# Taking the first expert layer's results back: stores by slot and gathers by pairs of columns in place of scatters and four block loads

## The chip, the cores and the metric

The kernel runs on one core of a Trainium2 chip. The metric is the device time of one execution in microseconds, the median of three runs. TensorE (PE), VectorE (DVE), ScalarE (ACT), GpSimd (POOL) and the DMA queues each work through their own list of instructions in order and wait for each other by semaphores, all of them written out by hand.

## What is computed

```python
h = concat([patches(x) @ proj_w.T + proj_b + pos, segment + sinusoid + token rows])   # 8 x 192 rows of 192
h = h + rotor_scan(layernorm(h))                          # a recurrence over the 192 positions
h = h + moe(layernorm(h), 8 experts, top 2, hidden 288, gelu)          # "experts(0)"
h = h + linear_attention(layernorm(h), 12 heads of 16)                 # relu(q), relu(k), k^T v, no softmax
h = h + moe(layernorm(h), 8 experts, top 2, hidden 768, silu)          # "experts(1)"
```

The 1536 token rows stand in SBUF as 12 columns of 128 rows: columns 0 to 3 hold the 64 image rows of two batch items each, columns 4 to 11 the 128 text rows of one item each. The attention of one item needs half an image column and one text column, so one "trio" (image column i, text columns 4 + 2i and 5 + 2i) is what two items need; there are four trios. `trio(i)` names them.

## The kernel before

**First experts.** `route(0)` on DVE gives each of the 3072 pairs (token row, chosen expert) a slot number. The slots are grouped by expert into 31 tiles of 128. POOL gathers a tile's rows from DRAM by an index list (`gather`, L738), PE transposes them, multiplies by the expert's two matrices, ACT applies the gelu, and DVE copies the result out of PSUM into one of eight buffers `ys` (`evac_y`, L1571). POOL then scatters the 128 result rows (`scatter`, L746) to the DRAM tensor `expert_rows` at the place of their token: choice 1 in the first 1536 rows, choice 2 in the next. On POOL's list gather and scatter alternate.

**Results back.** `load_acc` waits for all scatters and reads the rows back in token order with plain DMAs, four blocks of columns (`ACC`: 2, 2, 4 and 4 columns), choice 1 into `xn` on SP's queue and choice 2 into `a1` on ACT's. Behind its half, SP's queue holds the loads of the second experts' weights (L611 to L614, 9.4 MB). DVE multiplies both by the gates and adds them to `h` (L1630, two instructions a column), takes the statistics of the layer norm (`ln_start`, L1177 and L1180; `ln_end`, L1196 and L1197), ACT takes the square root (L821) and normalises (L834).

**Attention.** It works on six pairs of columns and four trios. For a pair, PE transposes the rows (`t_pair`, L1854), ACT copies them out (L1088), PE computes keys and values (`kv_mms`, L2229 and L2235), which DVE (`k_evac`, L1642) and ACT (`v_evac`, L1098) copy out; queries are computed for two pairs at a time (`q_mms`, L2261 and L2266, copied out by DVE in `q_evac`, L1650). For a trio there are the sums k^T v (`sums`, L2283 and L2289; DVE's `state`, L1660), numerator and denominator (`numden`, L2305 and L2310; DVE's `ratio`, L1673 to L1678), the transposes of the result (`t_att`, L2317; ACT's `att_evac`, L1118) and the output projection (`out_proj`, L2338; DVE's `add_att`, L1712 to L1180). The pairs go in the order of the columns, so the first text columns are the third pair, and the first `sums` stands behind the transposes of all six pairs. PE's list is written out at the end of `build`, DVE's above it.

**Behind it.** The next layer norm, the routing of the second layer on DVE and the 31 tiles of the second experts follow; POOL gathers and scatters there too. `keep_busy(n, b)` is n matmuls of 128x512 in bf16 whose result is not used (L1803).

## Time and profile before

| what | value |
|---|---|
| median of 3 runs (457.75 to 463.28) | 462.23 us |
| profiled execution, its own time | 462.79 us |
| its span, first to last instruction | 461.0 us |
| mean granted TensorE clock | 0.956 of full |
| busy: PE, DVE, ACT, POOL | 91%, 63%, 43%, 49% |
| first experts, first gather to last copied result | 137.5 to 230.9 us |
| results back and attention, to the end of the last projection | 230.9 to 298.6 us |
| layer norm and routing, to the first transposed row of the second experts | 298.6 to 320.8 us |
| second experts and the end | 320.8 to 461.0 us |

Times inside the execution are microseconds from the start of the span. In a row of the timeline the first number is the start, the second the duration; "x8" merges eight instructions that follow one another; the bracket at the end is the time for which the engine was idle before, and what ended it. SPq and ACTq rows are DMA issues.

### The profile page before, as it was taken

How to read it: one execution, taken by the hardware profiler on the slowest of the kernel's cores; microseconds unless marked ns; L12 is line 12 of the kernel's file. 1: busy time of each engine (PE TensorE's matmuls, PEld its weight loads, DVE VectorE, ACT ScalarE, POOL GpSimd, SP SyncE). 2: the span in 40 equal slices, each digit the busy share in tenths (PEclk: the TensorE clock that was granted, in tenths of full speed). 3: DMA queues.
4: the chain of work that ended last, by engine and by line, in shares of the span. 5: the costliest groups of instructions: out<-in, count | busy, mean ns of one | idle time of the engine just before them, and what ended most of it. 6: DMA issues, size and time to landing. Idle time of an engine off the chain costs nothing.

```text
span 461.0 us, 10231 instructions
## 1 busy us (share of the span) xinstructions
PE 420.2 (91%) x3568; PEld 326.3 (71%) x3568; DVE 292.3 (63%) x1360; ACT 197.3 (43%) x374; POOL 225.6 (49%) x266
## 2 busy tenths in 40 slices
PE   7999998989788988989987988977999999999993
PEld 5653655637536877878844557933999999999993
DVE  6579999999782433333558336887465566556651
ACT  1287945441751111110123401546566566566660
POOL 4302798797035666666520000334456665665544
PEclk9799799999989999898979999998999999999998
DMA  8609400010132122222169999079233233333322
GB/s 233 96 1 227 113 0 3 1 35 1 58 102 70 60 61 70 69 70 70 47 195 236 224 225 217 15 137 139 50 62 50 54 62 63 51 55 61 51 25 27
DMA packets 40128, 39.02 MB, mean 85 GB/s; under 512 B 7575, under 2 KB 37259, under 8 KB 40079
## 3 DMA queue, kind: packets, MB, share of 16 engines
q1 hardware_dynamic: 28861, 23.05, 22.5%
q0 software_dynamic: 9312, 14.03, 15.3%
q10 hardware_dynamic: 1906, 1.30, 1.0%
q8 instruction: 29, 0.48, 0.4%
q14 instruction: 20, 0.16, 0.1%
HBM read 28.00 MB, written 11.06 MB: 85 GB/s over the span
## 4 chain that ended last, share of the span: by engine, by line
PE 66%; DVE 11%; DMA 10%; ACT 4%; POOL 4%; issue 4%; POOLq 1%; SPq 0%; DVEq 0%; another core or an unknown queue 0%; ACTq 0%
PE bank L1955 11%; PE bank L1990 10%; PE bank L1941 7%; PE bank L1983 7%; DMA out<-a,idx 5%; PE bank L2036 4%; POOL reg L707 3%; PE bank L1803 3%; PE bank L1964 2%; DMA xn<-expert_rows 2%; PE bank L1918 2%; ACT xn L834 2%; DMA reg<-xn_rows,idxs 1%; PE bank L2229 1%; DMA reg<-in_patchT 1%
## 5 line engine op out<-in xcount | busy, mean ns | idle before, releaser
L738 POOL DMA_INDIRECT reg<-xn_rows,idxs x62 | 60.5, 976 | 30.3 <-issue 16.6
L1955 PE MATMUL bank<-reg,xT 64*128 64x128 f32 x1116 | 72.6, 275 | 1.4 <-issue 1.1
L758 POOL DMA_INDIRECT out<-a,idx x31 | 50.3, 1622 | 46.7 <-DMA out<-a,idx 35.8
L1955 PEld LDWEIGHTS bank<-reg,xT 64*128 64x128 f32 x1116 | 68.6, 188 | 1.5 <-issue 1.0
L1990 PE MATMUL bank<-reg 64*128 64x192 f32 x744 | 69.0, 323 | 0.0
L1990 PEld LDWEIGHTS bank<-reg 64*128 64x128 f32 x744 | 63.4, 187 | 0.0
L1803 PE MATMUL bank<-con 128*128 128x512 bf16 x201 | 55.3, 435 | 0.0
L1045 ACT ACTIVATE reg<-reg 128x1152 f32 x31 | 36.1, 1163 | 30.8 <-PE bank L1990 30.8
L1574 DVE TENSOR_SCALAR a<-bank,gs 128x192 f32<-128x192 f32 x31 | 13.0, 418 | 53.2 <-PE bank L1990 53.2
L1024 ACT ACTIVATE reg<-bank 128x288 f32<-128x288 f32 x31 | 12.5, 410 | 77.4 <-PE bank L1941 62.9
L746 POOL DMA_INDIRECT expert_rows<-a,idx x31 | 30.6, 986 | 25.2 <-DVE a L1571 19.1
L1803 PEld LDWEIGHTS bank<-con 128*128 128x128 bf16 x201 | 21.6, 111 | 27.6 <-issue 12.0
L1941 PE MATMUL bank<-reg,xTs 96*128 (+1 forms) x124 | 36.7, 418 | 4.8 <-DVE xTs L1537 4.7
L1983 PE MATMUL bank<-reg 96*128 x186 | 36.9, 336 | 0.3 <-issue 0.3
L1571 DVE COPY a<-bank 128x192 f32<-128x192 f32 x31 | 11.0, 354 | 39.6 <-PE bank L1983 20.6
L1983 PEld LDWEIGHTS bank<-reg 96*128 96x128 f32 x186 | 32.8, 195 | 3.7 <-issue 0.8
L1547 DVE TENSOR_SCALAR reg<-bank,gb 128x128 f32<-128x128 f32 x93 | 32.3, 403 | 0.0
L787 POOL TENSOR_SCALAR onep<-rs 128x3 f32<-128x3 f32 x4 | 0.9, 228 | 57.2 <-DVE nm L1189 57.2
L1941 PEld LDWEIGHTS bank<-reg,xTs 96*128 96x128 f32 (+1 forms) x124 | 21.8, 196 | 9.8 <-issue 6.2
L707 POOL TENSOR_TENSOR reg<-reg 128x128 f32<-128x128 f32 x63 | 26.1, 457 | 5.1 <-PE bank L2110 4.9
L1028 ACT ACTIVATE reg<-bank 128x384 f32<-128x384 f32 x31 | 15.2, 490 | 21.7 <-PE bank L1955 13.4
L1309 DVE TENSOR_REDUCE bank<-reg 128x6 f32<-128x24 f32 x176 | 23.9, 181 | 0.0
(363 smaller groups left out, 800.9 us busy)
## 6 DMA issues: line engine op xcount, KB each, us to landing
reg<-in_w2b SPq DMA_DIRECT2D x8, 576.0 KB, 10.2
reg<-in_w1b SPq DMA_DIRECT2D x8, 288.0 KB, 10.4
reg<-in_w1a SPq DMA_DIRECT2D x8, 216.0 KB
reg<-in_w2a SPq DMA_DIRECT2D x8, 216.0 KB
xn_rows<-xn SPq DMA_DIRECT2D x4, 384.0 KB, 2.7
reg<-in_w1b SPq DMA_DIRECT2D x8, 192.0 KB, 8.5
xn_rows<-xn SPq DMA_DIRECT2D x1, 1152.0 KB, 7.8
out<-h SPq DMA_DIRECT2D x1, 1152.0 KB
```

Of the source, the lines that this page charges most:

```text
L707: ins = nc.gpsimd.tensor_tensor(term[b % 2][k][:, 0:n, :, r, :], second[:, :, :, r, k:k + 1].to_broadcast([P, n, NCH, 4]), first[:, :, :, ...
L738: pool.indirect_dma_start(xs[:, i % RING, 0:(D, D2)[l]], None, xd[l], bass.IndirectOffsetOnAxis(ap=idxs[:, i:i + 1], axis=0)).then_inc(xs_ ...
L746: pool.indirect_dma_start(ybuf, bass.IndirectOffsetOnAxis(ap=idx2[:, i:i + 1], axis=0), ys[:, i % YRING, :], None).then_inc(scat[i % YRING ...
L758: pool.indirect_dma_start(out, bass.IndirectOffsetOnAxis(ap=idx2[:, i:i + 1], axis=0), ys[:, i % YRING, :], None, compute_op=ALU.add).then ...
L1045: nc.scalar.activation(w2r[:, p, :], w2b.rearrange("p e c n -> p (e c n)")[:, bass.ds(e * W2R, W2R)], ACT.Copy).then_inc(w2r_act, 1)
L1309: V.tensor_reduce(slot(t)[:, ch, 0:3], entries[:, ch], AX, ALU.add).then_inc(scan_self[half], 1)
L1547: ins = V.tensor_scalar(dst[:, k], src[:, :, 64 * k:64 * k + 64], gb2[:, 0, k:k + 1], gb2[:, 1, k:k + 1], ALU.mult, ALU.add)
L1803: MM(bank[bk][:, :], con[:, 0:P // 2].bitcast(BF16), con[:, 0:2 * P].bitcast(BF16), start=True, stop=True)
L1941: ins = MM(bank[2 + p][:, 0:hid], xTs[0:r, p, k, :], w1v[0:r, bass.ds(e * (NK * hid) + k * hid, hid)], start=(k == 0), stop=(k == NK - 1))
L1955: ins = MM(bank[2 + 2 * p + a][:, c * P:(c + 1) * P], w1r[rs, p, col:col + hc], xT64[rs, p, k, :], start=(c == 0 and k == 0), stop=(c == n ...
L1983: ins = MM(bank[6 + p][:, 0:D], hTs[0:r, p, c * P:(c + 1) * P], w2v[0:r, bass.ds(e * (nhc * D) + c * D, D)], start=(c == 0), stop=(c == nh ...
L1990: ins = MM(bank[Y_BANKS[i == NT - 1][a]][:, 0:D], hT2[rs, p, c * P:(c + 1) * P], w2r[rs, p, c * D:(c + 1) * D], start=(c == 0), stop=(c == ...
```

## The change

- `expert_rows` is now laid out by slot: tile i of the first experts is stored whole, 128 rows in a piece, by SP (a plain DMA for each of the 31 tiles, each waiting for `y_ev`). POOL's list in this layer holds the 31 gathers alone. The weight loads stand behind the stores on SP's queue.
- `load_acc` on SP and ACT goes. `results_back(n)` on POOL gathers the results of pair n by the slot numbers (`sli`), four indirect DMAs a pair (two columns, two choices), 24 in all. Pairs 2 to 5 first wait until the transposed rows of pair n - 2 have been copied out (`xT_ready`). Two of POOL's memsets stand between them.
- The pairs now go in batch order (`ORDER`): trio 0 is pair 0 and half of pair 1, and so on. `xn`, `a1`, `att`, `kb`, `vb`, `qT` and `attT` are indexed by that order.
- On PE, DVE and ACT the attention is written out anew: each pair's keys, each trio's sums and projections come as soon as their pairs are there. Keys and values of all pairs share banks 2 and 3; queries and sums share banks 4 and 5; the queries of the last two pairs are computed one pair at a time (`Q_PAIRS`), so there are four `q_mms` where there were three. PE has 12 more `keep_busy` matmuls after the landing of the first pair's last gather, and four after its first keys.
- The rows of the second layer's input are stored in two steps of six DMAs each in place of two DMAs.

```diff
-        ybuf = nc.dram_tensor("expert_rows", [TOPK * NTOK + 32 * P, D], F32, kind="Internal").ap()
+        ybuf = nc.dram_tensor("expert_rows", [NT * P, D], F32, kind="Internal").ap()
...
+        ND_BANK = [(6, 7), (6, 7), (6, 7), (2, 3)]
+        PR_BANK = [(6, 7), (6, 7), (6, 7), (4, 5)]
+
+        Q_PAIRS = ((0, 2), (2, 2), (4, 1), (5, 1))
...
+        ORDER = [j for i in range(NBP) for j in trio(i)]
+        GROUPS[3] = [ORDER[2 * n:2 * n + 2] for n in range(NPAIR)]
...
-            load_acc(sp, 0)
+
+            for i in range(NT):
+                sp.wait_ge(y_ev, i + 1)
+                sp.dma_start(ybuf[i * P:(i + 1) * P, :], ys[:, i % YRING, :]).then_inc(y_st[i % YRING], 16)
...
+            for i0, i1 in ((0, NBP - 1), (NBP - 1, NBP)):
+                sp.wait_ge(xn5_ready, 3 * i1)
+                of = xn[:, 3 * i0:3 * i1, :].rearrange("p (i v) n -> p i v n", v=3)
+                pat = slice(i0, i1)
+                for c, n in ((slice(0, D), D), (slice(D, DX), DX - D)):
+                    sp.dma_start(tok_rows(xd[1])[:, pat, c], of[:, :, 0, 0:n]).then_inc(xd_written, 16)
+                    for a in range(2):
+                        sp.dma_start(tok_rows(xd[1])[:, NPJ + 2 * i0 + a:NPJ + 2 * i1:2, c],
+                                     of[:, :, 1 + a, 0:n]).then_inc(xd_written, 16)
...
-                    if l == 0:
-                        pool.indirect_dma_start(ybuf, bass.IndirectOffsetOnAxis(ap=idx2[:, i:i + 1], axis=0),
-                                                ys[:, i % YRING, :], None).then_inc(scat[i % YRING], 16)
-                        return
...
+            def results_back(n):
+
+                for q in (2 * n, 2 * n + 1):
+                    for k, buf in enumerate((xn, a1)):
+                        a, g = k * NJ + ORDER[q], 2 * q + k
+                        if g >= YRING:
+                            pool.wait_ge(scat[g % YRING], 16 * (g // YRING))
+                        pool.indirect_dma_start(buf[:, q, :], None, ybuf,
+                                                bass.IndirectOffsetOnAxis(ap=sli[:, 0, a:a + 1], axis=0)
+                                                ).then_inc(scat[g % YRING], 16)
...
             route_share(0)
-            expert_dma(0)
-
-            wait_scatters(pool, 0)
+            first_dma()
+
+            wait_results(pool, y_st)
+            results_back(0)
             link(nc.gpsimd.memset(vb[:, :, KC:KV], 1.0))
+            results_back(1)
             nc.gpsimd.memset(attT[KC:KC + 1, 1, :], 1.0).then_inc(att_ones, 1)
+            for n in range(2, NPAIR):
+
+                pool.wait_ge(xT_ready, XT_BASE[3] + n - 1)
+                results_back(n)
 
...
-            load_acc(act, 1)
...
+            rows3(3)
+            ln_std(3, 4)
+            v_evac(3)
             att_evac(0)
+            rows3(4)
+            ln_std(3, 5)
+            v_evac(4)
+            rows3(5)
             att_evac(1)
             ln_std(4, 0)
             norm5(0)
+            v_evac(5)
             att_evac(2)
...
+                for g in range(4 * n, 4 * n + 4):
+                    dve.wait_ge(scat[g % YRING], 16 * (g // YRING + 1))
...
-            for g in range(2):
-                k_evac(g)
-                if g == 0:
-                    ln_end(3, 3)
-                q_evac(g)
+            rows_back(0)
+            ln_end(3, 0)
+            rows_back(1)
+            k_evac(0)
+            ln_end(3, 1)
+            rows_back(2)
+            k_evac(1)
+            ln_end(3, 2)
+            q_evac(0)
             state(0)
+            rows_back(3)
             k_evac(2)
+            ln_end(3, 3)
             ratio(0)
+            rows_back(4)
+            k_evac(3)
+            ln_end(3, 4)
+            q_evac(1)
+            before_att(0, 2, 3)
             state(1)
+            rows_back(5)
+            add_att(0)
+            k_evac(4)
+            ln_end(3, 5)
+            ratio(1)
+            ln_end(4, 0)
             q_evac(2)
-            ratio(1)
             state(2)
-            before_att()
-            add_att(0)
+            k_evac(5)
+            add_att(1)
             ratio(2)
+            before_att(2, 4, 6)
+            q_evac(3)
             state(3)
-            ln_end(4, 0)
-            add_att(1)
             ratio(3)
             ln_end(4, 1)
             shift(0, 2)
...
+            pe.wait_ge(scat[3], 16)
+            keep_busy(12, 6)
...
+            def rows_t(n, attended):
+
+                pe.wait_ge(xn_ready, 2 * NJ + 2 * n + 2)
+                pe.wait_ge(xT_ready, XT_BASE[3] + n - 1)
+                if attended:
+                    pe.wait_ge(at_ev, 2 * attended)
+                two = xn[:, 2 * n:2 * n + 2, :].rearrange("p j n -> p (j n)")
+                for v in range(3):
+                    ins = nc.tensor.transpose(bank[n % 2][:, v * P:(v + 1) * P], two[:, v * P:(v + 1) * P], ident)
+                ins.then_inc(xt_psum, 1)
...
+            def kv_mms(n):
+
+                pe.wait_ge(xT_ready, XT_BASE[3] + n + 1)
+                if n:
+                    pe.wait_ge(k_ev, n)
+                    pe.wait_ge(v_ev, n)
+                for a in range(2):
...
+                if c:
+                    pe.wait_ge(st_ev, c)
...
+                pairs = (3 * i + 2) // 2 + 1
+                pe.wait_ge(k_ev, pairs)
+                pe.wait_ge(v_ev, pairs)
+                pe.wait_ge(q_ev, 2 * i + 2)
...
-            for g in range(2):
-                kv_mms(g)
-                if g == 0:
-                    q_mms(0)
-                t_pair(3, 2 * g + 2)
-                t_pair(3, 2 * g + 3)
-                if g:
-                    q_mms(g)
+            rows_t(0, 0)
+            kv_mms(0)
+            keep_busy(4, 6)
+            rows_t(1, 0)
+            kv_mms(1)
+            q_mms(0)
+            rows_t(2, 0)
             sums(0)
             kv_mms(2)
             numden(0)
+            rows_t(3, 0)
+            kv_mms(3)
+            t_att(0)
+            q_mms(1)
             sums(1)
+            out_proj(0)
+            rows_t(4, 1)
+            kv_mms(4)
+            numden(1)
             q_mms(2)
-            t_att(0)
-            numden(1)
+            rows_t(5, 1)
+            t_att(1)
             sums(2)
-            out_proj(0)
-            t_att(1)
+            kv_mms(5)
+            out_proj(1)
+            q_mms(3)
             numden(2)
             sums(3)
-            out_proj(1)
             t_att(2)
             numden(3)
             out_proj(2)
```

POOL's list in the first experts and behind them, before (the columns are the line, the instruction, what it writes and reads, its shape and what it waits for):

```order
L738 DMA reg<-xn_rows,idxs 128x192 [waits tx_mm]
L746 DMA expert_rows<-a,idx 7168x192 [waits y_ev]
...
L746 DMA expert_rows<-a,idx 7168x192 [waits y_ev] x8
L781 MEMSET reg 128x24x6 [waits scat4,scat5,scat3,scat6,scat2,scat7,scat1,scat0]
L782 MEMSET reg 1x1536 [waits pool_self]
L787 TENSOR_SCALAR onep<-rs 128x3 [waits rstd_ready]
```

and now (`y_st` counts the stores, `scat` the landings of the gathers):

```order
L739 DMA reg<-xn_rows,idxs 128x192 [waits tx_mm] x27
L762 DMA xn<-expert_rows,sli 128x192 [waits y_st4,y_st5,y_st3,y_st6,y_st2,y_st7,y_st1,y_st0]
L762 DMA a<-expert_rows,sli 128x192
...
L799 MEMSET reg 128x24x6
L762 DMA xn<-expert_rows,sli 128x192 [waits pool_self]
...
L801 MEMSET reg 1x1536
L762 DMA xn<-expert_rows,sli 128x192 [waits scat0,xT_ready]
L762 DMA a<-expert_rows,sli 128x192 [waits scat1]
L762 DMA xn<-expert_rows,sli 128x192 [waits scat2]
L762 DMA a<-expert_rows,sli 128x192 [waits scat3]
```

The scatters are gone from between the gathers, and 24 gathers stand ahead of the normalisation's work.

DVE's list around the third copy of queries, before (ratio, the sums' state, queries, ratio):

```order
L1678 TENSOR_TENSOR a<-bank,z 128x384
L1660 TENSOR_TENSOR reg<-bank,con 96x204 [waits st_mm,att_ready]
L1660 TENSOR_TENSOR reg<-bank,con 96x204
L1650 TENSOR_SCALAR reg<-bank 96x2x2x128 [waits q_mm]
L1650 TENSOR_SCALAR reg<-bank 96x2x2x128
L1673 TENSOR_SCALAR z<-bank 128x24 [waits nd_mm]
```

and now:

```order
L1704 TENSOR_TENSOR a<-bank,z 128x384
L1216 RECIPROCAL rs<-sd 128x2x3 [waits std_ready,att_ready]
L1217 SCALAR_TENSOR_TENSOR nm<-mv,rs 128x2x3 [waits dve_self]
L1674 TENSOR_SCALAR reg<-bank 96x2x128 [waits q_mm]
L1674 TENSOR_SCALAR reg<-bank 96x2x128
L1685 TENSOR_TENSOR reg<-bank,con 96x204 [waits nd_mm,st_mm]
L1685 TENSOR_TENSOR reg<-bank,con 96x204
L1665 TENSOR_SCALAR reg<-bank 128x384 [waits kv_mm]
...
L1704 TENSOR_TENSOR a<-bank,z 128x384
L1718 TENSOR_TENSOR base<-lgx,std 128x48 [waits l3_ev,att_ready]
L1719 TENSOR_TENSOR corr<-rsum,mv 128x48
L1721 TENSOR_TENSOR base<-base,corr 128x48 [waits dve_self]
L1674 TENSOR_SCALAR reg<-bank 96x2x128 [waits dve_self,q_mm]
```

The queries' copy stands ahead of the sums' state now; the third stands behind the end of the next layer norm for trio 0 (L1216), the fourth behind a ratio and `before_att`.

PE's list between the second `numden` and the third `sums`, now:

```order
L2333 MATMUL bank<-reg 128x102 x4
L2285 MATMUL bank<-reg 96x128 [waits st_ev]
L2285 MATMUL bank<-reg 96x128 x3
L2290 MATMUL bank<-reg 96x128 x4
L2255 MATMUL bank<-con,xn 128x128 [waits at_ev,xT_ready,xn_ready]
L2255 MATMUL bank<-con,xn 128x128 x2
L2340 MATMUL bank<-con,a 96x128 [waits at_ev,xT_ready,att_ready]
...
L2304 MATMUL bank<-reg 96x102 [waits v_ev,q_ev,k_ev,att_ones]
```

and the part of before in which the sums' matmuls had no wait for queries (`q_ev`):

```order
L2310 MATMUL bank<-reg 128x102 x4
L2283 MATMUL bank<-reg 96x102 [waits v_ev,st_ev,k_ev,att_ones]
L2283 MATMUL bank<-reg 96x102 x3
L2289 MATMUL bank<-reg 96x102 x4
L2261 MATMUL bank<-reg 96x256 [waits q_ev]
```

Each `sums` is behind a copy of queries now, because both write banks 4 and 5.

## Rows read from the trace of the kernel before

**Rows 1.** Busy times by stretch, 241.90 to 298.70: sum over four stretches

```profile
sum 56.80, PE 50.41 PEld 35.60 DVE 35.30 ACT 18.83 POOL 3.39; mean PE 12.60 PEld 8.90 DVE 8.82 ACT 4.71 POOL 0.85
```

**Rows 2.** Timeline, PE, 241.9 to 298.7: all rows with idle time before them

```profile
243.10 1.58 PE L2229 MATMUL bank<-reg 128*128 128x392 f32 x4 [0.58 <-ACT reg L1088]
246.50 0.55 PE L1854 MATMUL bank<-con,xn 128*128 128x128 f32 x3 [1.82 <-ACT xn L834]
255.11 1.55 PE L2229 MATMUL bank<-reg 128*128 128x392 f32 x4 [1.09 <-ACT reg L1088]
270.97 0.58 PE L2305 MATMUL bank<-reg 96*64 96x102 f32 x8 [1.35 <-ACT reg L1098]
278.26 0.39 PE L2317 MATMUL bank<-con,a 128*96 128x128 f32 x2 [1.48 <-DVE reg L1650]
```

**Rows 3.** Timeline, end of the first experts: last result, last scatter, its landing

```profile
230.53 0.36 DVE L1571 COPY a<-bank 128x192 f32<-128x192 f32 x1 [0.64 <-PE bank L1983]
...
231.44 0.97 POOL L746 DMA_INDIRECT expert_rows<-a,idx  x1 [0.30 <-DMA expert_rows<-a,idx]
...
234.01 0.22 POOL L781 MEMSET reg<- 128x144 f32 x1 [1.60 <-DMA expert_rows<-a,idx]
```

**Rows 4.** Timeline, the first two columns from their landing to PE

```profile
237.41 0.75 DVE L1630 SCALAR_TENSOR_TENSOR h<-xn,gate,h 128x192 f32<-128x192 f32 x2 [0.85 <-DMA a<-expert_rows]
...
239.63 0.25 DVE L1180 BATCH_NORM_AGGREGATE mv<-st 128x2 f32<-128x6 f32 x2
...
241.97 0.55 PE L1854 MATMUL bank<-con,xn 128*128 128x128 f32 x3
```

**Rows 5.** A gather's landing: chain of waits at 317.70; the eight of token rows

```profile
317.70 2.94 DMA reg<-xn_rows,idxs
```

```profile
DMA to landing us min/median/max: 4.5/4.7/4.8
```

**Rows 6.** DMA issues: queue, count, KB each, median us to landing

```profile
a<-expert_rows ACTq DMA_DIRECT2D x2, 384.0 KB, 8.8
xn<-expert_rows SPq DMA_DIRECT2D x2, 384.0 KB, 8.5
```

**Rows 7.** Chain of waits (start, us): queries, and keys with values, of one step

```profile
260.70 1.73 PE bank L2261 x8
262.43 1.04 PE bank L2266 x8
...
264.87 1.51 PE bank L2229 x4
266.38 0.86 PE bank L2235 x4
```

**Rows 8.** Timeline, DVE: copies of keys and of queries, and one ratio

```profile
257.57 0.56 DVE L1642 TENSOR_SCALAR reg<-bank 128x384 f32<-128x384 f32 x1 [0.45 <-PE bank L2235]
...
276.83 1.28 DVE L1650 TENSOR_SCALAR reg<-bank 96x512 f32<-96x512 f32 x2 [1.97 <-PE bank L2266]
...
292.11 0.18 DVE L1673 TENSOR_SCALAR z<-bank 128x24 f32<-128x24 f32 x1
...
292.81 0.82 DVE L1678 TENSOR_TENSOR a<-bank,z 128x192 f32<-128x192 f32 x2
```

**Rows 9.** Timeline, PE: the last output projection

```profile
296.32 2.31 PE L2338 MATMUL bank<-prw,reg 96*128 96x200 f32 x12
```

**Rows 10.** Timeline, first experts: PE's second product, and two late result copies

```profile
170.90 0.36 DVE L1571 COPY a<-bank 128x192 f32<-128x192 f32 x1 [2.35 <-PE bank L1983]
...
177.80 1.14 PE L1983 MATMUL bank<-reg 96*128 x6
...
180.30 1.14 PE L1983 MATMUL bank<-reg 96*128 x6
...
182.94 0.36 DVE L1571 COPY a<-bank 128x192 f32<-128x192 f32 x1 [3.77 <-PE bank L1983]
...
184.84 1.86 PE L1983 MATMUL bank<-reg 96*128 x6
```

More of the change, by code:

```diff
@@ L66 @@
 YRING = 8
+SCAT0 = NA // YRING
 NV = 2
@@ L88 @@
 NCONST = NCON0 + 2 * P
-LANDED = [16 * (sum(1 for n in range(NT) if n % YRING == (i - 1) % YRING) + (i - 1) // YRING + 1) if i else 16
+LANDED = [16 * (SCAT0 + (i - 1) // YRING + 1) if i else 16
           for i in range(32)]
@@ L1850, in t_pair @@
                     pe.wait_ge(xT_ready, m + q - 1)
-                if n == 3:
-                    two = xn[:, 2 * q:2 * q + 2, :].rearrange("p j n -> p (j n)")
-                    for v in range(3):
-                        ins = nc.tensor.transpose(bank[q % 2][:, v * P:(v + 1) * P], two[:, v * P:(v + 1) * P], ident)
-                    ins.then_inc(xt_psum, 1)
-                    return
                 for k in range(NK):
```

309 lines of the change are left out of this document (131 added, 178 removed).

## The prediction

> **What bounds the kernel now.** I read the table of the stages first, then the busy times of the stretch that the change rewrites, then PE's idle rows in it, and last the rows that lead into it and out of it. The reader is to see four things.
>
> First, the stretch from 241.97 us, when PE transposes the first rows that came back [rows 4], to 298.63 us, when the last output projection ends [rows 9], is 56.7 us long, and PE is busy for 50.4 of 56.8 us [rows 1]. The five rows in which PE was idle give the rest: 0.58 + 1.82 + 1.09 + 1.35 + 1.48 = 6.3 us [rows 2]. So PE bounds this stretch, although its first `sums` stands behind all six pairs. A reordering can't win more here than those 6.3 us; only an earlier start can.
>
> Second, what sets the start. The last result is in `ys` at 230.53 + 0.36 = 230.9. The last scatter is issued at 231.44, lands 2.35 us later, and POOL goes on at 234.01 [rows 3]. The loads go out then, and the first two columns are there at 237.4. From there to the first transpose it takes 4.56 us [rows 4].
>
> Third, behind the last projection DVE's chain (statistics, top two, ranks, slots) leads to the second experts with no part in which the change does anything. I let it ride rigidly on the last projection. SP's twelve stores of rows in place of two, at an estimated half a microsecond each, cost some 3 us more behind the last trio, and lie under that chain: the gather that needs them goes out at 317.70 [rows 5], 19 us behind the last projection. Were the cover gone, it would cost the 3 us of the last six.
>
> Fourth, the first experts. PE passes from tile to tile in 180.30 - 177.80 = 2.50 us, but every fourth result copy on DVE is late, and the period of four tiles is 182.94 - 170.90 = 12.04 us instead of 10.0 [rows 10]. What causes it the rows don't show; I come back to it among the rivals.
>
> **The change, part by part.**
>
> *Scatters off POOL, stores on SP.* 31 indirect DMAs go from POOL and 31 plain ones come to SP, which has nothing else to do there. PE sets the pace of this stage, so I cost it at nothing until the end of the stage. There, POOL's last three scatters ran one behind the other. A store can go out right at 230.9. No store of this shape into `expert_rows` is in the trace; with the scatter's 2.35 us of landing it is there at 233.2, and POOL goes on 0.2 later, at 233.4. That is 0.6 us earlier than before. Its bounds are a landing of nothing (233.4 becomes 231.1) and twice the scatter's (235.7).
>
> *Gathers for block loads.* Four indirect DMAs bring a pair. POOL's rows have 0.97 us each and 0.30 between [rows 3], 1.27 from start to start. So the fourth of pair 0 starts at 233.4 + 3 x 1.27 = 237.2. Its landing is bounded by 2.94 us (a gather of the second experts, beside few other DMAs) and 4.8 us (the slowest of the eight gathers of token rows, beside the first loads) [rows 5]. The weights' loads run beside all 24 of these, and they start earlier than before. The two halves of the block load, on two queues, landed after 8.8 and 8.5 us [rows 6]: the queues shared evenly, 1152 KB each in about 8.7 us. At that rate the 96 KB of a gather take 0.7 us, and alone about half as long, so I take 2.94 + 0.4, about 3.4 us, nearer the low end. Pair 0 is there at 240.6.
>
> The Trainium skill has a rule on just this ("DMA: Bandwidth & Descriptors", section "Queues, rings and completion order"): each DMA engine goes round robin between the queues that have work, a packet at a time. By it a gather is held up by a packet of weights for each of its own and not by the megabytes queued ahead, and the trace's even halves agree; without it, in one common line with 9.4 MB of weights, pair 0 would land tens of us later.
>
> From landing to the first transpose it was 4.56 us before; now the second block doesn't come between on DVE, which saves 0.3. First transpose: 240.6 + 4.3 = 244.9, against 241.97. **Start: +2.9 us.** PE's 12 extra `keep_busy` matmuls lie in this wait and end before it.
>
> *PE's own work.* The same instructions in another order, but for one thing: queries of 256 tokens took 1.73 + 1.04 = 2.77 us [rows 7], and the third such step becomes two of 128 tokens. The same weights are loaded twice and half as many columns stream. Bounds are half each (nothing added) and 2.77 each (+2.8). I take 1.8 each. **Work: +0.85 us.** The four `keep_busy` (0.9 us) stand in a wait.
>
> *PE's waits, in the order of its list.* The steps have these lengths: a pair's rows need on DVE 239.88 - 237.41 = 2.5 us from landing to the end of the statistics, then some 1.8 us through ACT to PE [rows 4], then 0.6 us until PE may use the transposed rows [rows 2]; keys and values take 1.51 + 0.86 = 2.4 us [rows 7], their copy 0.6, queries' copy 1.3 [rows 8].
>
> 1. Keys of pair 0 wait for the copy of the transposed rows: 0.6. They run from 246.0 to 248.4.
> 2. Pair 1's gathers are at POOL behind pair 0's and a memset: fourth at 242.6, landed at 246.0, statistics until 248.5. Now `k_evac(0)` stands ahead of `ln_end(3, 1)` on DVE, and its keys ended at 248.4. The rows are at PE at 250.7. Wait 2.3, and 0.6 for the copy.
> 3. Pair 2 waits at POOL until pair 0's rows are copied out, 246.0; fourth gather 249.8, landed 253.2, at PE 257.9. PE ended its first queries at 256.9: wait 1.0.
> 4. Pair 3's gathers (from 251.8, landed by 259.0) aren't what is late: DVE first does `state(0)`, whose sums end at 259.7. Then 0.6 + 2.5 + 0.6 for `k_evac(2)`, and the way to PE: 265.1, where PE was free at 263.7. Wait 1.4, and 0.6 for the copy.
> 5. Pairs 4 and 5 land at 266.1 and 273.3, before DVE comes to them. The gathers and their pacing cost nothing from here; each has 0.6 for the copy: 1.2.
> 6. `sums(1)` stands right behind `q_mms(1)` and waits for its copy: 1.4, as `t_att(0)` did [rows 2].
> 7. `sums(2)` waits for the third copy of queries, and on DVE that stands behind `ln_end(4, 0)`. This needs ACT's root, which stands behind `att_evac(1)`, which needs PE's `t_att(1)`, the instruction just ahead of `sums(2)`. From its end: 0.1, two copies 0.8, two roots 0.6, `ln_end` 0.4, queries' copy 0.75: wait 2.6.
> 8. `sums(3)` waits for the fourth copy, on DVE behind `ratio(2)`, which needs `numden(2)`, again the instruction just ahead: 0.1, ratio 292.81 + 0.82 - 292.11 = 1.5 [rows 8], three small additions at 0.18 each, 0.75: wait 3.0.
>
> The sum is 0.6 + 2.3 + 0.6 + 1.0 + 1.4 + 0.6 + 1.2 + 1.4 + 2.6 + 3.0 = 14.7 us, against 6.3 before. **Waits: +8.4 us.** The pieces for ACT in item 7 are estimates from the same steps elsewhere; all ten items together could be 4 us less (where DVE is earlier than I laid it out) or 3 us more.
>
> **Sum.** 2.9 + 0.85 + 8.4 = 12.1 us more. The profiled execution took 462.79 us, 0.56 above the median of the runs, within their spread of 457.75 to 463.28. 462.79 + 12.1 = 474.9 us.
>
> **Rivals.**
>
> *A, slower still.* Gathers land after 4.8 us instead of 3.4, which delays pairs 0, 1 and 2 in a row, since pair 2 is gated by pair 0: +2.8. And TensorE's clock falls in the new waits. After the late copy at 182.94 six matmuls took 1.86 us instead of 1.14 [rows 10], and such a tile 1.7 us more; two of the waits above are longer than the one there. With one or two falls: 474.9 + 2.8 + 2 to 3.4 = 480 to 481. For it: the longest new waits, 2.6 and 3.0. Against it: behind PE's wait of 1.82 in the old stretch the transposes took 0.55 us, as they had before it [rows 2, 4].
>
> A rule of the Trainium skill speaks for still slower gathers ("SBUF — State Buffer", in the section on the peaks of the ports, the trap it calls "DVE blocks DMA"): while DVE runs a copy in its two-port mode, GpSimd can't write the descriptors of its DMAs. The trace has POOL at 0.97 us for each while DVE copies from PSUM [rows 3], so I give it no more than A's share.
>
> *B, the late copies of the first experts go away; not slower.* Before, POOL had two DMAs for each tile, 2 x 1.27 = 2.54 us, a little more than PE's 2.50. If POOL's load is the cause and 31 DMAs fewer remove it, five periods of four tiles give back 2.04 us each, 10 us: 462.79 + 12.1 - 10.2 = 464.7, within 2%. It decides from the point at which POOL has slack in a tile, which it would have at 1.27 us. Against it: the late copies wait on neither POOL nor a DMA by the rows; what ended them is put down to PE.
>
> *C, the batch order does what its shape suggests.* If the waits of items 2, 4, 7 and 8 overlap with work that I laid behind them, the stretch has the old 6.3 us of idle: 462.79 + 2.9 + 0.85 = 466.5, within 2%. Together with B it would be 456, faster by 1.4%, not by 2. For it: sums and projections no longer wait for the sixth pair. Against it: PE was busy anyway, so nothing was waiting that this sets free.
>
> *D, the change does nothing:* gathers wholly under PE's `keep_busy`, 462 to 463. Against it: the first loads landed at 237.4 and four gathers can't be issued and landed by then.
>
> **How the numbers follow.** A difference under 2% (9.2 us) is about what a measurement of this kernel can't tell from none. My sum, with bounds of -4 and +5 for the landing of the store and gathers, the queries and the waits, gives 471 to 480: chance 0.51. A: 0.12. B: 0.14. C: 0.12, D: 0.03. B and C together, or the same with more: 0.08. Of the sum's own 0.51, 0.02 falls under the 2% bound of 471.5. So slower 0.61, same 0.33, faster 0.06 (the part of B and C together that gains more than I gave it). The predicted time is the sum's, 474.9; its own range is 471 to 480; the range that leaves out no more than 2 in 10 is 463 to 481.
>
> **What would show it.** In the profile after: pair 0's last gather issued at about 237 and landed between 240 and 242; the first transposed rows at 244 to 247; PE idle before the sums' matmuls (L2304) twice by 2.5 to 3 us, ended by DVE's copy of queries; PE's busy time in the stretch about 51 to 52 us; the last projection ending near 310.7. POOL's gathers of pairs 4 and 5 would stand well ahead of DVE's use of them. The forecast is wrong if the first experts' period of four tiles is near 10 us, if DVE's L1657 waits for landings at pair 4 or 5, or if the two long waits before `sums` aren't there.

## The result, and the profile after

The changed kernel takes 480.04 us (median of 4 runs, 476.29 to 481.02), the kernel before 460.46 us on the same chip (457.75 to 463.28): 1.041 times as long, 95% interval 1.032 to 1.050. That is slower, 5.1 us above the predicted 474.9 and inside its range of 463 to 481. Every ratio here leaves out an execution that took over 1.5% longer than the fastest of its kernel.

The sum came out near for reasons that are partly others than those predicted. The table of the stages shows it. First the busy times by stretch of the kernel after (columns: stretch, its length, busy time of each engine with its instructions, granted TensorE clock, DMA share, GB/s):

```profile
137.50:215.70 78.20, 77.17 (x461) 68.56 (x459) 35.56 (x92) 13.91 (x32) 24.85 (x27) 1.00 0.24 73
215.70:234.30 18.60, 13.41 (x50) 6.90 (x50) 4.63 (x23) 1.28 (x3) 9.16 (x10) 0.74 0.99 238
234.30:317.00 82.70, 66.55 (x348) 46.72 (x349) 38.58 (x150) 20.62 (x56) 18.97 (x25) 0.81 0.43 100
317.00:478.20 161.20, 148.98 (x2134) 138.54 (x2132) 93.59 (x346) 91.25 (x148) 87.09 (x71) 0.96 0.37 64
```

The page's slices say the same for the whole span: the clock sags around the middle, from the stretch in which the DMA engines are full (DMA 8 and 9) to well behind it.

```profile
span 478.2 us, 10334 instructions
...
PEclk9999899999899999997888797688999999999998
DMA  8629000000422222218999300047223333333313
```

The executions that were profiled differ by 478.2 - 461.0 = 17.2 us. By stages, before and after:

| stage | before | after | difference |
|---|---|---|---|
| to the first gather of token rows | 137.5 | 131.8 | -5.7 |
| from there to the last result copy | 93.0 | 83.5 | -9.5 |
| last result copy to first transposed rows | 11.4 | 19.0 | +7.6 |
| first transposed rows to the end of the last projection | 56.7 | 82.6 | +25.9 |
| behind it | 162.4 | 161.3 | -1.1 |

The first line is no effect of the change that I can name. In the 14 profiles of this study that point lies between 131.8 and 137.6 us, behind code that hardly changes; the profile of after has the earliest and that of before one of the two latest. The granted clock up to there was 0.98 after and 0.93 before. Without that line these two executions differ by 22.9 us; the medians differ by 19.6.

The second line is rival B. In the kernel before, every fourth result copy was late [rows 10]. Now DVE's timeline has one every 2.50 us, and the last few, of which the third row is the last, come closer still:

```profile
179.43 0.36 DVE L1595 COPY a<-bank 128x192 f32<-128x192 f32 x1 [1.35 <-PE bank L2011]
...
181.93 0.36 DVE L1595 COPY a<-bank 128x192 f32<-128x192 f32 x1 [1.35 <-PE bank L2011]
...
215.32 0.36 DVE L1595 COPY a<-bank 128x192 f32<-128x192 f32 x1 [0.64 <-PE bank L2011]
```

The third line is a slow gather. These are the last of pair 0's four gathers on POOL, PE's idle time until it is there, DVE's first use of the rows, and the first transposes:

```profile
221.91 0.95 POOL L762 DMA_INDIRECT a<-expert_rows,sli  x1 [0.30 <-issue]
...
229.96 4.02 PE L1837 MATMUL bank<-con 128*128 128x512 bf16 x12 [3.39 <-DMA a<-expert_rows,sli]
...
230.05 0.75 DVE L1657 SCALAR_TENSOR_TENSOR h<-xn,gate,h 128x192 f32<-128x192 f32 x2 [8.78 <-DMA a<-expert_rows,sli]
...
234.32 0.72 PE L2255 MATMUL bank<-con,xn 128*128 128x128 f32 x3 [0.33 <-ACT xn L857]
```

The reader is to see 230.05 - 221.91 = 8.1 us from issue to use, where the prediction had 3.4, and `keep_busy` (L1837) at 4.02 us for 12 matmuls: 0.34 us each, where full clock gives 0.22.

The fourth line is the largest. All rows of PE with an idle time of half a microsecond or more, from the first transposes to the last projection:

```profile
235.62 1.58 PE L2265 MATMUL bank<-reg 128*128 128x392 f32 x4 [0.58 <-ACT reg L1110]
...
240.19 0.55 PE L2255 MATMUL bank<-con,xn 128*128 128x128 f32 x3 [1.15 <-ACT xn L857]
241.32 2.79 PE L2265 MATMUL bank<-reg 128*128 128x392 f32 x4 [0.58 <-issue]
...
252.04 0.90 PE L2255 MATMUL bank<-con,xn 128*128 128x128 f32 x3 [3.71 <-ACT xn L857]
...
260.26 0.55 PE L2255 MATMUL bank<-con,xn 128*128 128x128 f32 x3 [1.07 <-ACT xn L857]
261.38 2.38 PE L2265 MATMUL bank<-reg 128*128 128x392 f32 x4 [0.58 <-ACT reg L1110]
...
270.45 0.92 PE L2304 MATMUL bank<-reg 128*96 128x102 f32 x8 [1.48 <-DVE reg L1674]
...
276.71 1.58 PE L2265 MATMUL bank<-reg 128*128 128x392 f32 x4 [0.58 <-ACT reg L1110]
...
283.32 0.40 PE L2340 MATMUL bank<-con,a 128*96 128x128 f32 x2 [0.63 <-issue]
...
286.72 1.65 PE L2304 MATMUL bank<-reg 128*96 128x102 f32 x8 [2.57 <-DVE reg L1674]
...
301.86 0.92 PE L2304 MATMUL bank<-reg 128*96 128x102 f32 x8 [3.21 <-DVE reg L1674]
```

They add up to 16.1 us, against 6.3 before [rows 2]. That explains 9.8 of the 25.9 us. The rest stands in the busy time, 66.55 us against 50.41 [rows 1]: the same four matmuls of L2265 take 1.58 us at 2.4 GHz, and 2.79 or 2.38 in rows over which the granted clock is 0.54 and 0.65, so mostly at the lower level, 1.2 GHz. The granted clock of the stretch is 0.81, where it was 1.00 at every point of the old one.

### The profile page after: what moved, and what is told of

The parts are those of the page before. It is cut to its first block, busy times and chain, and to the rows that moved or that the text cites. A ratio compares the mean times of both kernels' runs of the same rounds, so it can differ in the third digit from the quotient of the medians.

```text
span 478.2 us, 10334 instructions
## 1 busy us (share of the span) xinstructions
PE 430.1 (90%) x3600; PEld 332.8 (70%) x3600; DVE 291.2 (61%) x1364; ACT 198.2 (41%) x376; POOL 217.7 (46%) x259
## 4 chain that ended last, share of the span: by engine, by line
PE 37%; DMA 23%; DVE 18%; issue 8%; POOL 7%; ACT 6%; POOLq 1%; DVEq 0%; ACTq 0%
DMA out<-a,idx 19%; PE bank L2011 6%; PE bank L1969 6%; DVE bank L1337 4%; DVE reg L1330 3%; PE bank L1837 3%; PE bank L2361 3%; PE bank L1992 2%; POOL reg L710 2%; PE bank L1983 2%; ACT xn L857 2%; DMA a<-expert_rows,sli 2%; PE bank L2265 1%; PE bank L1946 1%; POOL reg L720 1%
## 5 line engine op out<-in xcount | busy, mean ns | idle before, releaser
L739 POOL DMA_INDIRECT reg<-xn_rows,idxs x62 | 59.8, 965 | 58.3 <-PE bank L1946 33.5
L1837 PE MATMUL bank<-con 128*128 128x512 bf16 x217 | 57.9, 425 | 3.4 <-DMA a<-expert_rows,sli 3.4
L1837 PEld LDWEIGHTS bank<-con 128*128 128x128 bf16 x217 | 22.8, 109 | 32.8 <-issue 11.5
L2011 PE MATMUL bank<-reg 96*128 x186 | 35.3, 325 | 0.6 <-DVE reg L1586 0.6
L1969 PE MATMUL bank<-reg,xTs 96*128 (+1 forms) x124 | 35.4, 406 | 0.4 <-issue 0.4
L2011 PEld LDWEIGHTS bank<-reg 96*128 96x128 f32 x186 | 31.6, 189 | 4.1 <-issue 1.1
L762 POOL DMA_INDIRECT xn<-expert_rows,sli x12 | 11.6, 963 | 39.8 <-DMA expert_rows<-a 19.8
L844 ACT ACTIVATE std<-mv,con 128x2 f32<-128x2 f32 (+2 forms) x11 | 3.3, 296 | 49.6 <-DVE mv L1208 46.2
```

Source lines behind the costliest of these rows:

```text
L739: pool.indirect_dma_start(xs[:, i % RING, 0:(D, D2)[l]], None, xd[l], bass.IndirectOffsetOnAxis(ap=idxs[:, i:i + 1], axis=0)).then_inc(xs_ ...
L1837: MM(bank[bk][:, :], con[:, 0:P // 2].bitcast(BF16), con[:, 0:2 * P].bitcast(BF16), start=True, stop=True)
L1969: ins = MM(bank[2 + p][:, 0:hid], xTs[0:r, p, k, :], w1v[0:r, bass.ds(e * (NK * hid) + k * hid, hid)], start=(k == 0), stop=(k == NK - 1))
L2011: ins = MM(bank[6 + p][:, 0:D], hTs[0:r, p, c * P:(c + 1) * P], w2v[0:r, bass.ds(e * (nhc * D) + c * D, D)], start=(c == 0), stop=(c == nh ...
```

## The experiments

Twelve kernels were run. Ratios are to executions of the kernel before taken beside them; the changed kernel's own is 1.041. They are estimated from the single executions and aren't exactly the quotients of the medians: for h1 the medians, 484.79 and 462.44, would give 1.048.

| run | time, us | ratio (95%) |
|---|---|---|
| e1_stores | 450.99 | 0.976 (0.969 to 0.983) |
| e2_weights_late | 466.63 | 1.012 (1.003 to 1.022) |
| e3_fill | 474.27 | 1.026 (1.019 to 1.033) |
| e4_dve_order | 473.69 | 1.025 (1.018 to 1.032) |
| e5_late_and_dve | 459.10 | 1.000 (0.996 to 1.004) |
| f1_gathers_old_order | 476.73 | 1.038 (1.034 to 1.043) |
| f2_gathers_weights_late | 472.05 | 1.029 (1.023 to 1.035) |
| h1_no_pacing | 484.79 | 1.056 (1.046 to 1.066) |
| h2_late_dve_no_pacing | 468.43 | 1.015 (1.008 to 1.022) |
| k1_shorter_lead | 483.39 | 1.048 (1.042 to 1.055) |
| g1_half_scatters | 453.52 | one execution |
| g2_all_scatters | 462.40 | one execution |

**Stores alone.** In the kernel before, POOL's scatters are replaced:

```
+            for i in range(NT):
+                sp.wait_ge(y_ev, i + 1)
+                sp.dma_start(ybuf[i * P:(i + 1) * P, :], ys[:, i % YRING, :]).then_inc(y_st[i % YRING], 16)
             load_acc(sp, 0)
```

> The kernel before with one part of the change alone: SP stores each result tile plainly by its slot, POOL keeps only its gathers of xn_rows in the first experts, and the rest (block loads, attention in the old order) stays. It leaves out the order of the results: the block loads read the rows as the slots lie, so the values behind them are other ones. Theory 1 (POOL's two DMAs for each tile, 2.54 us beside PE's 2.50, make every fourth result copy late): the result copies come every 2.50 us, the last is issued at 215.3 as in the changed kernel instead of 230.5, and with the store landing in 1.6 us instead of 2.35 the time is 462.8 - 15.2 - 1 = 446 to 449 us. Rival (the late copies go with something else of the changed kernel, such as the layout or what stands in PE's list): the period of four tiles stays near 12 us and the time is 459 to 463 us.

The time is 450.99 us, 12 us under that of before and 2 us above the expected 446 to 449. DVE waits for PE alone before its 31 result copies, and they take 217.7 - 146.8 = 70.9 us from first to last, where before they took 230.5 - 149.7 = 80.8:

```profile
L1582 DVE COPY a<-bank x31: 357/358/358, 146.8 to 217.7; 128x192 f32<-128x192 f32 x31
its engine sat idle before it (us, times) until:
  PE bank L1994: 39.1, 31
```

So the stores win about 10 us, as rival B had it (10.2), and it is the scatters' leaving that wins them.

**How many scatters it takes.** Two kernels, executed once each, put scatters back that nobody reads, first for every second tile, then for every tile:

```
-                    if l == 0:
+                    if l == 0 and not (i % 2 == 0):     (g2: i >= 0)
                         return
```

> The kernel of e1_stores (block loads, stores by SP into rows of their own) in which POOL again scatters the results of every second tile, into rows that nobody reads; the values behind the loads are other ones, as there. POOL has then 1.5 DMAs for each tile, 1.9 us beside PE's 2.50. Theory 1 (the late copies come when POOL has no slack in a tile, 2.54 against 2.50 us): the copies come every 2.50 us and the last one at 215 to 218. Rival (each so many scatters hold DVE's copy up, whatever slack POOL has): 3 to 4 late copies remain, the stage is 6 to 8 us longer, and the last one comes at 222 to 226.

> The kernel of g1_half_scatters with the scatter of every tile back on POOL (again into rows that nobody reads, SP's stores stay, the values behind the loads are other ones). Theory 1 (POOL's slack in a tile decides: 2.54 us of issues beside 2.50 us of PE): the late copies are back at every fourth tile, a period of four tiles of 12 us, and the last copy comes 80 us or more behind the first one, against 70.5 us with half of the scatters. Rival (the late copies go with something else that SP's stores took away, such as the wait for the scatter's landing before a slot of the ring is used again): the copies stay at 2.50 us, 71 to 72 us from first to last.

The result copies of the one and of the other, first and last start:

```profile
L1593 DVE COPY a<-bank x31: 344/358/359, 147.5 to 218.0; 128x192 f32<-128x192 f32 x31
```

```profile
L1593 DVE COPY a<-bank x31: 344/357/358, 146.2 to 228.1; 128x192 f32<-128x192 f32 x31
its engine sat idle before it (us, times) until:
  PE bank L2005: 20.1, 11
  issue: 9.3, 10
  remote: 8.9, 3
```

Half of the scatters cost nothing (70.5 us), all of them 11.4 us (81.9), although SP's stores stayed. It is no price for each scatter; it appears between 1.5 and 2 DMAs of POOL for each tile of 2.50 us. One execution each is enough for this, since the copies' times are read from the profile; the whole times, 453.52 and 462.40 us, agree.

**The lead of the gathers.** In the kernel before, one number:

```
-                ahead = RING + (3, 2)[l]
+                ahead = RING + (1, 2)[l]
```

> The kernel before with one number changed: in the first experts POOL's gathers of token rows run five tiles ahead of the scatters instead of seven. The count of POOL's DMAs stays. Theory 1 (what makes the copies late is POOL's load alone): the period of four tiles stays near 12 us and the time is 457 to 462 us. Rival (it is the order in POOL's list, a scatter behind a gather that waits for its ring slot): the late copies go, and the time is 445 to 450 us. Second rival (with a shorter lead PE waits for gathers): over 462 us.

The second rival, and strongly: 483.39 us. Among the waits of 150 to 225 us PE now has one for the gathered rows themselves, 15 times (the profiled execution took 490.07 us, 6.7 more than the median, so I read only which waits there are):

```profile
PEld bank L1918 <- DMA reg<-xn_rows,idxs: 25.5, 15, 2.6
...
PE bank L1918 <- DMA reg<-xn_rows,idxs: 21.1, 15, 2.3
```

The count of POOL's DMAs was the same, so the lead matters beside the load. What the late copies of before wait for in detail isn't settled by this.

**Weights held back.** In the changed kernel SP waits ahead of the second experts' weights:

```
+            for s in range(YRING):
+                sp.wait_ge(scat[s], 16 * SCAT0)
             for e in range(NE):
                 part = w1b[:, e, :].rearrange("p (k f) -> p k f", k=NK3)
```

> The changed kernel with SP's loads of w1b and w2b (9.4 MB) held until all 24 gathers of results have landed. Theory 1 (the gathers land after 8 us because they share the DMA engines with these loads, which the windows show at a DMA share of 1.1): landing falls from 8 us to 3 to 3.5; the first transposes come at 229.5 to 230 instead of 234.3; the wait before pair 2's transposes falls from 3.71 us to about 1; all in all 7 to 8 us less, and up to 3 more where TensorE's clock then stays up: 469 to 473 us. Rival (the gathers are slow by themselves, or DVE's copies hold POOL's descriptors back): landing stays at 7 us or more and the time is within 1 us of 480.

466.63 us, 13 us less and more than the 7 to 11 that I expected. The last gather of pair 0 on POOL, and DVE's first use:

```profile
224.22 0.95 POOL L764 DMA_INDIRECT a<-expert_rows,sli  x1 [0.31 <-issue]
```

```profile
226.91 0.75 DVE L1659 SCALAR_TENSOR_TENSOR h<-xn,gate,h 128x192 f32<-128x192 f32 x2 [3.63 <-DMA a<-expert_rows,sli]
```

The landing is 2.7 us, against 8.1. The first transposes come 13.7 us behind the last copy instead of 19.0; the stretch behind them is 71.6 us instead of 82.7, with 57.3 us of PE busy at a granted clock of 0.93. So the landings cost 5.3 us at the start, and with them went a good part of the clock's loss: PE's busy time in the stretch is 9.2 us less. PE's waits in it are still 14.3 us (71.6 - 57.3), of which the 2.57 and 3.21 before the sums are unchanged; the wait before pair 2's transposes fell from 3.71 to 0.16. The weights arrive later and are still in time: the rest behind the last projection is 161.9 us, as after the change.

**PE kept busy.**

```
+            keep_busy(16, 6)
             rows_t(2, 0)
...
+            pe.wait_ge(k_ev, 5)
+            pe.wait_ge(v_ev, 5)
+            keep_busy(11, 2)
             sums(2)
...
+            pe.wait_ge(k_ev, 6)
+            pe.wait_ge(v_ev, 6)
+            keep_busy(14, 2)
             sums(3)
```

> The changed kernel with keep_busy matmuls in PE's three longest waits: 16 ahead of pair 2's transposes, 11 ahead of sums(2), 14 ahead of sums(3), at 0.22 us each at full clock 3.5, 2.4 and 3.1 us, about as long as the waits. Theory 1 (the waits are what lets the granted clock fall to half; PE's busy time of 66.6 us between the first transposes and the last projection is 51 us at full clock): the granted clock of that stretch rises from 0.81 to 0.93 or more and the time falls by 8 to 14 us, to 466 to 472. Rival (the clock falls for another reason, and the fill only lengthens PE's list): clock about 0.8 and 480 to 486 us.

The clock did what was expected, the time only half of it:

```profile
235.90:311.90 76.00, 65.65 (x385) 44.13 (x390) 38.51 (x150) 19.34 (x53) 18.73 (x24) 0.93 0.47 109
```

The clock is 0.93 instead of 0.81. PE's 41 extra matmuls take some 9 of the 65.65 us, which leaves 57 us for the same work that took 66.6. The stretch is 6.7 us shorter, and the time, 474.27 us, is 5.8 us less and above the expected 466 to 472. Work that filled the waits held the clock higher here, but the waits' time stays in PE's list.

**DVE's order.**

```
-            ln_end(4, 0)
             q_evac(2)
+            ln_end(4, 0)
...
-            ratio(2)
-            before_att(2, 4, 6)
             q_evac(3)
+            ratio(2)
+            before_att(2, 4, 6)
```

> The changed kernel with two copies of queries moved ahead on DVE: the third ahead of ln_end(4, 0), the fourth ahead of ratio(2) and before_att(2, 4, 6). Theory 1 (sums(2) and sums(3) wait for these copies behind DVE's other work, items 7 and 8 of the prediction): PE's waits before L2304 fall from 2.57 and 3.21 us to 0.5 and 1.4 (what a queries' copy itself takes behind its matmuls), 3 to 4 us less, and more where the clock stays up: 470 to 477 us. Rival (the transposes of the attention's rows, which need ratio and att_evac, are late next and take the wait over): 478 to 481 us.

473.69 us, and the two long waits are gone; PE's rows of the third and fourth `sums`:

```profile
285.09 0.87 PE L2304 MATMUL bank<-reg 128*96 128x102 f32 x8
...
294.15 0.92 PE L2304 MATMUL bank<-reg 128*96 128x102 f32 x8
...
297.24 0.58 PE L2328 MATMUL bank<-reg 96*64 96x102 f32 x8 [0.60 <-DVE reg L1685]
```

I had expected 0.5 and 1.4 us of them to be left. Nothing of size took their place, only 0.60 us before the next step. The stretch fell from 82.7 to 68.2 us: some 5 us of waits and some 9 us of clock (PE busy 57.05 instead of 66.55). The time fell by only 6.3 us by the medians. This kernel's profiled execution, with 469.4 us, is the fastest of its five, so I trust the medians for the size.

**Both together.**

> The changed kernel with two edits that helped it alone: the weights' loads held until the 24 gathers have landed (13.4 us less alone), and the third and fourth copies of queries moved ahead on DVE (6.4 us less alone, of which 5 are PE's waits). Theory 1 (landings and DVE's order are separate causes, the rest of either gain is clock, and it can be won once only): 459 to 463 us, the kernel before's time within 2%. Rival (the gains add in full): 457 to 460. Rival (one hides the other): 465 or more.

459.10 us (10 runs) beside 459.43 (13 runs): the kernel before's time. The stretch from the first transposes to the last projection:

```profile
230.60:291.60 61.00, 52.63 (x349) 36.90 (x348) 38.36 (x149) 19.42 (x53) 19.67 (x25) 1.00 0.66 157
```

459.10 us lies in the range of Theory 1 and in that of the first rival, so the time doesn't tell them apart. PE's busy time does: each edit alone took off 9.2 and 9.5 us of it, both together 13.9, so part of either gain can be won only once.

The clock is full. This one row gives the bill of the changed kernel's stretch: the same matmuls need 52.63 us at full clock, so 66.55 - 52.63 = 13.9 us of its busy time was clock. And with landings short and DVE in a better order PE still waits 8.4 us.

**The first half of the change with the old attention.** The 24 gathers in place of the block loads, in the kernel before with SP's stores, and then with the weights held as well:

```
+            for g, ab in enumerate(ACC):
+                for j in range(*ab):
+                    for k, buf in enumerate((xn, a1)):
+                        a = k * NJ + j
+                        pool.indirect_dma_start(buf[:, j, :], None, ybuf,
+                                                bass.IndirectOffsetOnAxis(ap=sli[:, 0, a:a + 1], axis=0)
+                                                ).then_inc(acc_ld[g], 16)
```

> The kernel before with the first half of the change alone: stores by slot on SP, 24 gathers on POOL in place of the block loads, in the columns' own order, and the attention in its old order (all six pairs first). The weights' loads start as early as before. Theory 1 (the change loses by its order of the attention, with its waits of 14.7 us and the clock that they cost, and by the landings of 8 us; the stores give back 15 us): the first transposes come 19 us after the last result copy as in the changed kernel instead of 11.4, then 57 to 60 us to the end of the last projection: 461 - 14 + 7.6 + 2 = 455 to 459 us. Rival (the gathers alone set the pace, whatever the order behind them: 24 x 1.27 us and 8 us of landing): PE waits for columns 4 to 11 as well, the stretch is 65 us or more, and the time is 462 or more.

> The same with the loads of w1b and w2b held until all 24 gathers have landed. Theory 1 (the landings are long only for these loads): the first transposes come 13.7 us after the last result copy, as where the changed kernel's loads were held, and the time is 5 to 6 us less than that of the run beside it: 450 to 454 us, faster than the kernel before by more than its measurement is uncertain. Rival (the loads then come late for the second experts, or all six pairs wait for POOL's 30 us of gathers): no gain, 455 us or more.

Both expectations failed, by 18 us and more: 476.73 and 472.05 us, where the rivals had 462 or more and 455 or more. Only the difference between the two, 4.7 us for the held loads, is near the 5 to 6 that I had. PE's first long waits with the weights held:

```profile
231.45 0.90 PE L1872 MATMUL bank<-con,xn 128*128 128x128 f32 x3 [5.14 <-ACT xn L853]
...
242.32 0.90 PE L1872 MATMUL bank<-con,xn 128*128 128x128 f32 x3 [6.41 <-issue]
```

Gathers come at 5 us for a pair, and the old order wants groups of 2, 2, 4 and 4 columns, each with its last step behind the next group's first sums on DVE. From e1_stores to f1 the differences are the gathers and the values in the rows, and they cost 6.2% (1.038 - 0.976), some 29 us; with the weights held as well it is 5.3% (1.029 - 0.976), some 24 us. So gathers in place of block loads lose with the old order too. With the weights held and DVE's order untouched the new order has 1.012 (e2) and the old one 1.029 (f2). But f1 and f2 have no pacing either, and the next experiment shows that this can cost: the new order without it, with DVE's edit, has 1.015 (h2). So the new order isn't what makes the change lose; how much better it is by itself isn't shown.

**Without the pacing.**

```
-                pool.wait_ge(xT_ready, XT_BASE[3] + n - 1)
                 results_back(n)
```

> The changed kernel without the wait that gives the change its pacing: pairs 2 to 5 are gathered as soon as POOL comes to them. Theory 1 (the gate on pair 0's transposed rows, passed at 235.84, is what makes pair 2 late, since the gather behind it takes 8 us to land beside the weights): pair 2 is issued from 229.5 on and is there about 6 us earlier, PE's wait of 3.71 us before its transposes goes to 0.6 or less, and 3 to 6 us are won: 474 to 477 us. Rival (more gathers in flight beside the weights only land later, or DVE's order is late next at the same place): 479 to 481 us.

> The kernel of e5_late_and_dve (weights held, DVE's copies moved) without the pacing as well. There the gate opened 0.7 us behind POOL's last work before it, and DVE waited 3.41 us for pair 2. Theory 1 (the pacing costs only where the landings are slow): at most 0.7 us less, 458 to 459.5 us. Rival (POOL's 24 gathers in one run delay what DVE or the weights need): 460 or more.

Nothing was won. With the weights late it is 1.015, where the pacing had 1.000, and the rival holds. With them early it is 1.056, where the pacing had 1.041, more than even the rival had; but these two intervals overlap (1.046 to 1.066 and 1.032 to 1.050), so there only the missing gain is clear. In the second kernel POOL issues its 24 gathers without a pause from 220.37 to 251.88. PE ends the first queries and the transposes of pair 2 before 247 us. Then nothing of PE, DVE or ACT runs for some 8 us:

```profile
246.41 0.55 PE L2256 MATMUL bank<-con,xn 128*128 128x128 f32 x3
256.28 1.64 PE L2305 MATMUL bank<-reg 128*96 128x102 f32 x8 [9.32 <-DVE reg L1675]
```

```profile
254.85 1.28 DVE L1675 TENSOR_SCALAR reg<-bank 96x512 f32<-96x512 f32 x2 [10.66 <-remote]
```

```profile
254.90 0.49 ACT L1111 ACTIVATE reg<-bank 128x384 f32<-128x384 f32 x1 [9.51 <-remote]
```

```profile
250.93 0.95 POOL L764 DMA_INDIRECT a<-expert_rows,sli  x1 [0.30 <-issue]
```

DVE waits there only for PE's queries, ACT only for PE's transposes, and both go on within 0.05 us of each other. POOL's gathers go on at 1.25 us each until 251.88, and the stall lasts 3.0 us longer. In h1 DVE stands for 11.12 us in the same way, and PE for 11.88; there it goes on while POOL is in its last gather. In this stretch no profile with the pacing has a wait of DVE or ACT that ends with "remote". But a run of 24 gathers without a pause isn't enough to bring the stall about. POOL issues them so in f1 and f2 too: f1 has one such wait, of 3.60 us, and f2 has none.

```profile
253.59 0.38 DVE L1196 BATCH_NORM_AGGREGATE mv<-st 128x2 f32<-128x6 f32 x4 [3.60 <-remote]
```

## Why the prediction came out as it did

**Start, +2.9 us: the step on the landing failed.** I took 2.94 + 0.4 = 3.4 us, since the weights' packets would only share the engines. It measured 8.1 us beside the weights and 2.7 with them held. Rival A's 4.8 was too little as well. From the last result's end to the first transposes it is 18.6 us, where I had 244.9 - 230.9 = 14.0; with the weights held it is 13.3. The rest of the step was right: the store lands in 1.6 us (I had 2.35), POOL goes on 2.5 us behind the last copy's end as in the sum, and four gathers take 4 x 1.25 us. The 0.4 also came from a misread row: the 8.8 and 8.5 us [rows 6] are one load's way from issue to landing. The four loads of a half were issued over 2.2 us, so its 1152 KB took some 10 us and not 8.7. That is a small part of the miss.

By the rule of the Trainium skill that I cited ("DMA: Bandwidth & Descriptors", section "Queues, rings and completion order"), each DMA engine goes round robin between the queues, a packet at a time. I concluded from it that a gather is delayed only by the packets between its own. The trace agrees that it doesn't wait for the 9.4 MB, but the 5.4 us more are many times the 0.4 that I made of it.

**PE's own work, +0.85 us: right. The clock, put at nothing in the sum: a second step that failed.** At full clock the stretch has 52.63 us busy against 50.41; 1.0 of the 2.2 are the four `keep_busy`, the rest, 1.2, is near the 0.85. But I assumed full clock, and that cost 13.9 us. I had this in rival A, at 2 to 3.4 us, and with an argument against it, that the clock had held behind a wait of 1.82 us. One short wait in a busy stretch was no measure for eleven of them. How much the waits I had foreseen cost by themselves is nearest in e2: 14.3 us of waits (I had 14.7) with short landings, and 57.32 - 52.63 = 4.7 us lost to the clock. The other 9.2 us went with the slow landings.

**Waits, 14.7 us: the sum was near (16.1), its items less so.** Items 6, 7 and 8 were 1.4, 2.6 and 3.0; they measured 1.48, 2.57 and 3.21. For the last two DVE's order is shown to be the cause: they are gone in e4, where the first is still 1.68. Item 4 was 1.4 (1.07). Item 2 was 2.3 (1.15), too pessimistic. Item 3 was 1.0 and measured 3.71: POOL's gate on pair 0 opened at 235.84, and the gather behind it took 8 us to land. Item 5 said that pairs 4 and 5 land before DVE comes to them. Pair 4 didn't, DVE waited 4.47 us for it, and I had named this as a sign against me. My own times spoke against it: `numden(0)` ends at 263.7 (item 4) and a ratio takes 1.5 (item 8), so DVE was free at 265.2, ahead of the 266.1. It cost PE nothing: its transposes of pair 4 start at 275.58 without a wait.

```profile
265.52 0.75 DVE L1657 SCALAR_TENSOR_TENSOR h<-xn,gate,h 128x192 f32<-128x192 f32 x2 [4.47 <-DMA a<-expert_rows,sli]
```

**First experts, nothing: wrong.** I gave rival B a chance of 0.14 and 10.2 us. It came true, with 9.9 us from first to last copy, and was another of my signs against the forecast. My argument against it, that the rows put the late copies down to PE, was a weak one: between one late copy and the next POOL had issued with 0.30 us between its DMAs, and that was to be seen.

**The sum.** My 12.1 us for start, work and waits are, from the last copy on, 7.6 + 25.9 = 33.5 us. That is 21.4 more than I had. By the table rival B's stage gives back 9.5, and another 5.7 + 1.1 us lie ahead of and behind what the sum treats, which I can't put down to the change: 474.9 + 21.4 - 9.5 - 6.8 = 480.0 us, where the profiled execution took 480.2. So large errors of opposite sign left the forecast 5 us off, and that it came so near was luck.

**What the change is worth, part by part.** Stores in place of scatters: 10 us won, shown by e1, g1 and g2. Gathers in place of block loads: lost more than that, some 29 us with the old order (f1 against e1). Of the kernels run with gathers, only the one with the weights held and DVE's order mended reaches the time of before. No kernel here beats both: e5 is level with before, and e1_stores, with 451 us, doesn't bring the rows back in order. What a version with stores, short landings and cheaper gathers could reach stays open.

## What to carry to other kernels

When a change puts small transfers on the critical path, look at what else is in the queues at that moment, and hold back what isn't needed yet; here that was worth 13 us. Price new waits twice, once for themselves and once for TensorE's clock behind them, and don't expect the second price to be in proportion. Eleven waits of 16.1 us went with 13.9 us more in slow matmuls, 14.3 us of waits with short landings (e2) with 4.7, and 8.4 us (e5) with none. And an engine that issues DMAs without a pause is a warning in itself, even where nothing is seen to wait for it.

## What was not expected of the hardware

A gather of 128 rows of 768 bytes landed after 2.7 us with the loads held (e2) and after 8.1 us beside loads that kept the DMA engines at a share of 1.0 to 1.1.

In some kernels in which POOL issues indirect DMAs without a pause, DVE and ACT go on late from results that PE has long written by the profile: by 8 us and more in h1 and h2, and by some 2 us at every fourth tile where POOL has 2 DMAs of 1.27 us for 2.50 us. With 1.5 DMAs for each tile, or with the pacing, whose pauses are 0.7 us and more (e5), it is gone. In f2, though, 24 gathers without a pause brought no such wait. The releaser is "remote", so what holds the results back isn't in the profile. The Trainium skill knows the reverse ("SBUF — State Buffer", the trap "DVE blocks DMA"): there DVE's copy keeps POOL from writing descriptors. In h2's stall DVE runs nothing, ACT stands as well and POOL's DMAs land at their pace, so that trap doesn't cover it. That POOL's run of DMAs has a part in it is shown by adding and removing it (g1 and g2, e5 and h2); what else it takes, and which way it acts, is open.
